# Mixture-of-experts block: the experts' first layer in two column strips of 64 features and 64 tokens

## The reference

```
aff    = x @ centroids.T ; e = argmax(aff) ; alpha = sigmoid(aff[e])
h      = layernorm(x, ln_g[e], ln_b[e])
h      = relu(h @ w1[e].T + b1[e])          # 256 -> 1024
ye     = x + h @ w2[e].T + b2[e]            # 1024 -> 256
out    = alpha * ye + (1 - alpha) * x
```

## Time and profile before

| | us |
|---|---|
| median of 2 runs | 948.38 (948.35 to 948.42) |
| the profiled execution | 948.4 |
| its span, first to last instruction | 946.3 |
| TensorE busy | 870.7 (92%) |
| VectorE busy | 603.1 (64%) |
| ScalarE busy | 534.9 (57%) |
| GpSimd busy | 315.7 (33%) |

### The profile page before, as it was taken

How to read it: one execution, slowest core, us unless ns; L and a number is a source line. 1 busy time by engine, 2 the same in 40 slices (tenths; PEclk the granted TensorE clock), 3 DMA queues, 4 the chain that set the end, 5 groups by cost and what they waited for, 6 DMA issues and landing times. The chain is left out here.

```text
span 946.3 us, 20352 instructions
## 1 busy us (share of the span) xinstructions
PE 870.7 (92%) x6606; PEld 517.7 (55%) x6655; DVE 603.1 (64%) x1111; ACT 534.9 (57%) x1338; POOL 315.7 (33%) x471
## 2 busy tenths in 40 slices
PE   7999869999999999999999989924999999999996
PEld 4555413333333333333333326613999999999996
DVE  5888999888888888888888306861333333323332
ACT  4667437777777877877777874661322232232221
POOL 9988644333332232232333321461111111111111
PEclk9999979999999999999999999966999999999998
DMA  7588442422521112222213207345666566656660
GB/s 263 168 255 248 143 130 96 157 69 69 169 69 47 48 49 65 69 68 69 69 56 105 90 1 240 122 165 204 211 192 210 194 197 193 219 185 199 199 212 6
DMA packets 55139, 130.68 MB, mean 138 GB/s; under 512 B 9753, under 2 KB 30874, under 8 KB 48794
## 3 DMA queue, kind: packets, MB, share of 16 engines
q1 hardware_dynamic: 49482, 108.19, 36.7%
q0 software_dynamic: 5584, 21.54, 6.0%
HBM read 101.21 MB, written 28.48 MB: 137 GB/s over the span
## 5 line engine op out<-in xcount | busy, mean ns | idle before, releaser
L802 ACT ACTIVATE arena<-ps_pair 128x512 f32<-128x512 f32 (+3 forms) x768 | 328.9, 494 | 102.2 <-PE ps_pair L1134 94.7
L891 DVE TENSOR_REDUCE B_block_max<-ps_item 128x8 f32<-128x1024 f32 x288 | 340.5, 1220 | 40.9 <-PE ps_item L1041 37.8
L1134 PE MATMUL ps_pair<-q_stack,k_stack 99*128 99x512 bf16 (+5 forms) x720 | 182.3, 330 | 12.4 <-ACT arena L802 6.8
L717 POOL TENSOR_SCALAR_AFFINE_SELECT arena<-arena 128x256 f32<-128x256 f32 x256 | 103.9, 406 | 202.6 <-ACT arena L802 200.2
L1150 PE MATMUL ps_pair<-arena,B_v_quad 128*32 128x512 f32 (+3 forms) x1536 | 163.6, 498 | 1.0 <-ACT B_oacc L816 0.7
L1134 PEld LDWEIGHTS ps_pair<-q_stack,k_stack 99*128 99x128 bf16 (+1 forms) x768 | 54.0, 97 | 187.4 <-ACT arena L802 170.2
L1686 PEld LDWEIGHTS D_ps_h<-D_xT,arena 128*128 128x128 f32 x1248 | 147.8, 195 | 4.6 <-ACT D_xT L1624 2.7
L1686 PE MATMUL D_ps_h<-D_xT,arena 128*128 128x128 f32 x1248 | 148.3, 278 | 2.1 <-ACT D_xT L1624 2.1
L1705 PE MATMUL D_ps_y<-arena,D_hr 128*128 x624 | 141.0, 379 | 0.0
L1615 ACT ACTIVATE D_hr<-D_ps_h,ffn_columns 128x128 f32<-128x128 f32 x156 | 44.5, 368 | 165.4 <-PE D_ps_h L1686 165.4
L1598 POOL DMA_INDIRECT out<-D_res,D_ids x39 | 38.4, 984 | 259.5 <-issue 200.9
(11 more groups left out here) (163 smaller groups left out, 730.6 us busy)
## 6 DMA issues: line engine op xcount, KB each, us to landing
arena<-in_w_exp SPq DMA_DIRECT2D x39, 1024.0 KB
qk_parts<-arena SPq DMA_DIRECT2D x32, 384.0 KB, 3.5
q_stack<-qk_parts SPq DMA_DIRECT2D x96, 128.0 KB, 3.0
rows<-payload SPq DMA_DIRECT2D x39, 257.0 KB, 2.7
arena<-in_x SPq DMA_DIRECT2D x16, 512.0 KB, 6.2
k_stack<-qk_parts SPq DMA_DIRECT2D x64, 128.0 KB, 3.0
arena<-in_w_exp POOLq DMA_DIRECT2D x8, 1024.0 KB, 6.8
arena<-in_x_feat SPq DMA_DIRECT2D x8, 512.0 KB, 5.8
```

What stands on the lines that cost most here:

```text
L717: pool.affine_select(out=block_p, in_=block_p, compare_op=ALU.is_ge, fill=0.0, base=0, pattern=[[0, 2], [1, P]], channel_multiplier=-1).th ...
L802: act.activation(pr[s % PR][:, h, 0:QW - off], ps_s[(QH * s + j) % R][:, 0:QW - off], ACT.Exp, scale=scale).then_inc(s_e, 1)
L891: dve.tensor_reduce(bmx[:, g:QH:GH, first:first + 3 * gap + 1:gap], src[:, :, :].rearrange("p c (b n) -> p c b n", n=P), AX.X, ALU.max).th ...
L1134: pe.matmul(ps_s[(QH * s + j) % R][:, 0:QW - off], ks[rows, r, half, bass.ds(g * SEQ + kb * P, P)], qs[rows, r, half, bass.ds(g * SEQ + c ...
```

## The change

The product of a block of 128 features and 128 tokens becomes products of 64 features and 64 tokens. The array is used as two column strips of 64 columns; strip 0 holds features 0 to 63 of the block and strip 1 features 64 to 127. In the first turn strip 0 moves tokens 0 to 63 and strip 1 tokens 64 to 127, in the second turn the other way round. The semaphores stay where they were.

```
-                            for c in range(DC):
-                                at = c * FF + f * P
-                                mm = pe.matmul(ps_h[f // HC][:, f % HC, :], w1b[:, r, at:at + P], xT[:, r, c, :],
-                                               start=(c == 0), stop=(c == DC - 1))
+                            for turn in range(2):
+                                for c in range(DC):
+                                    for strip in range(2):
+                                        lo, at = HALF * ((strip + turn) % 2), c * FF + f * P + HALF * strip
+                                        mm = pe.matmul(ps_h[f // HC][HALF * strip:HALF * (strip + 1), f % HC, lo:lo + HALF],
+                                                       w1b[:, r, at:at + HALF], xT[:, r, c, lo:lo + HALF],
+                                                       start=(c == 0), stop=(c == DC - 1), tile_position=(0, HALF * strip))
```

## The result

| | before | changed |
|---|---|---|
| median, us | 948.38 (2 runs) | 1006.03 (1005.42 to 1006.64, 2 runs) |
| ratio, 95% interval | | 1.061 (1.056 to 1.065) |
| span of the profiled execution, us | 946.3 | 1003.5 |

Slower, as forecast, but by 6.1% and not by 3.4%: 1006.0 lies just outside the range that ended at 1005. The direction and most of the terms held; 25 us are missing from the sum.

The account below looks back on a forecast made before the run. The prediction took TensorE alone to bound the experts' stage, 7.25 us a slot. Terms 0.14 + 0.30 + 0.38 = 0.82 us a slot, over 39 slots +32.1 us on 948.4, gave 980.5 us, range 958 to 1005.

Parts of the forecast that it names:

- streaming, 64 rounds: Experts' first layer, L1686: 64 rounds of 0.058 us take 3.71 us against 3.57, +0.14 us a slot.
- changes of shape: Into strips before L1686 and out before L1695: two changes of array shape plus exposed loads, +0.30 us a slot.
- sequencer's lead, dry time: Before L1705: a lead of 36 records covers only 0.52 us, so TensorE runs dry, +0.38 us a slot.
- The strips run side by side: L1686: two strips work at once, inferred from the attention's four strips of 32 features running together.
- taken turns: Rival at L1686: strips alternate, 7.1 us instead of 3.57, +3.8 us a slot, 1096 us; chance 0.07.
- A round of 0.058 us: L1686: a round of two strips takes half of 0.107 us plus 0.005, loading balancing streaming.
- 0.10 us for a change of shape: Cost of each switch between full-width array and strips, read from L1150 and L1499 to L1507, without exposed loads.
- Semaphores, other engines, DMAs: Experts' stage: no wait added, relus have idle time, loads for next slots have more time; zero cost.
- The sequencer stays ahead: Rival: the sequencer's lead grows with two strips, the 0.38 us falls away, +17 us, 965.6 us; chance 0.13.
- independent arrays: Rival: strips load while the last full-width product drains, only streaming counts, -3 us, 945 us; chance 0.03.
- The hand-out is the bound: Rival at L1686: the sequencer's pace of handing out instructions limits, a slot of 10.0 us, 1056 us; chance 0.08.
- The loop's code: Rival: the experts' loop body of five blocks is not kept and is reread, +43 us, 1024 us; chance 0.07.

Follow-up runs that it names:

- f1: The changed kernel run again as it is, in the third job: 976.02 us, ratio 1.033 to the kernel before.
- e5: The changed kernel with GpSimd's result store moved beside the second layer and the expert's number read ahead of the first: 962.59 us, ratio 1.019.
- e4: The changed kernel without turns: two strips of 64 features, each moving all 128 tokens, in 32 products a slot: 958.03 us, ratio 1.009.
- e3: The changed kernel with TensorE's read of the expert's number moved ahead of the first layer: 980.98 us, ratio 1.033.
- e1: The changed kernel with GpSimd's store of a slot's result held until the first layer is done, beside the second layer: 980.25 us, ratio 1.033.
- g1: The changed kernel run a third time as it is, in the fourth job: 974.4 us, ratio 1.030 to the kernel before.

## Why the prediction was right and wrong

Term by term, a slot, in us. "Without the hole" is f1 against the kernel before, split by e5:

| term | forecast | measured |
|---|---|---|
| streaming, 64 rounds | +0.14 | +0.16 (0.0583 a round) |
| changes of shape | +0.30 | +0.30 (e5's +0.461 less the 0.16) |
| sequencer's lead, dry time | +0.38 | +0.34 (f1's 8.049 less e5's 7.706) |
| sum | +0.82 | +0.80 |
| indirect store against TensorE's supply of records | 0 | 0 or +0.69 to +0.74, by job |

- *The strips run side by side.* Right: had they taken turns, the first layer would have been over 7 us.
- *A round of 0.058 us.* Right to 0.0003. In L1686 a pair came every 0.112 us with 128 columns and 128 tokens; both halves scaled. The steps to it from L1150 and L1062, strips of 32 columns at the earlier trace rows, carried over to 64.
- *0.10 us for a change of shape.* Right: in the changed kernel L1708's last record starts 0.31 us before L1688's first (0.216 before), and L1688's last 0.15 before the transposes (0.112 before, with a pair twice as long). e4 costs +0.224 with the same two changes and rounds of 0.109.
- *The sequencer.* Right in place, cause and size: e3 takes the read of the expert's number away and with it all of the wait. The lead of 36 records held too: 18 pairs in all but one slot of the loop in e1, f1 and g1. e3 was run in a job with the hole, e5 in one without, and neither has the wait.
- *Wrong: "Semaphores, other engines, DMAs", which was put at zero.* I asked what waits for what, and found nothing added. GpSimd's store of the results does not come up in that step at all, and I did not ask what else could act on TensorE's supply of instructions. In the kernel before, the sequencer has its first layer handed out at 733.9, with 18 pairs of 0.112 us, 2.0 us, in hand, and L1598 starts a microsecond later (timeline of GpSimd, kernel before):

```profile
734.90 0.98 POOL L1598 DMA_INDIRECT out<-D_res,D_ids  x1 [6.32 <-issue]
```

With pairs of 0.029 us the same lead is 0.52 us, and the sequencer is still in the middle of handing out when the store starts. In a job where the indirect DMA holds up the supply, the lead is used up, 0.38 us go inside the first layer (4.266 against 3.883), and since the sequencer comes to the end of the layer only 3 to 10 pairs ahead instead of 18, another 0.31 us ahead of the second (0.826 against 0.520). 39 x 0.69 = 26.8 us is what the sum lacked (it was 0.02 us a slot too high elsewhere). What exactly is held up stays open. It is not the sequencer as such: in the kernel before, whose trace has the long waits of the jobs with the hole, the sequencer starts the eight register operations of L1705 from 735.0 to 735.9, about 0.13 us apart, while the store runs from 734.90 to 735.88. The forecast itself, 980.5, stands against 976.0 and 974.4 where nothing holds the supply up, ratios of 1.033 and 1.030 for its 1.034. Which of the two a run met was decided by the job and by nothing that the prediction weighed; but a sign of it stood in the trace of the kernel before, in the 6.3 us before L1518, which I had not looked into.
- *The rivals.* "The sequencer stays ahead" and "independent arrays" fell with f1. "The hand-out is the bound" fell as stated: e1 and f1 hand out 256 records at 14.6 ns each and keep their lead. The 62 ns per MATMUL that the Trainium skill ("TensorE: Matmul & The Clock Gate", "Wait — 56ns, not 53.3ns?") states for hardware decode off do not apply here: 128 MATMULs take 3.73 us, 29 ns each. But its place was the right one to look at: the missing term is a supply of records that stops at times. The loop's code stayed: TensorE's instruction reads, changed kernel, 700 to 950 us:

```profile
q8 instruction: 3, 0.05, 0.1%
```

Three blocks of 16 KB, against the over 30 that reading the body of five blocks in each of some seven passes would take. Of the two sizes in the Trainium skill ("Runtime: NRT & Kernel Launch", "Instruction fetch mechanics"), 2048 instructions agrees with this and two blocks does not.

## What to carry to other kernels

When a change cuts the same TensorE work into more and shorter instructions, count the sequencer's lead in time and not in instructions: 36 records were 2.0 us of cover before and 0.52 after, and everything that this cover had hidden (a register read, its operations, another engine's DMA) can come out at once. Move such reads ahead of the dense stretch (e3: -0.62 us a slot), and keep GpSimd's indirect DMAs beside long matmuls (e1: -0.68 in a job with the hole). When a time differs between jobs, look for a wait that differs too, also in stages that the change leaves alone. No variant here beats the kernel before: strips bring nothing where full-width products already stream and load side by side, and e5, the best with turns, is still 1.9% slower.

## What the runs showed that I had not expected

An indirect DMA of GpSimd, 0.98 us long, can hold up the supply of instructions to TensorE, which shares no semaphore or data with it: a hole of mostly 0.28 to 0.41 us behind a lead of 0.52, and with two in a row a slot of 10.15 us instead of 8.79, 0.30 of it by the lower clock of some second layers. It did so in every slot of some jobs and in none of others, for the same program, 1006 us and 976. The kernel before differs by only 0.5% between such jobs, about what the longer waits in the routing stage make; in its experts' stage, where the sequencer is 2.0 us ahead, every slot of the middle takes 7.245 us and no store shows.
